# Fused attention and feed-forward layer: fp32 transposes in tiles of 64 rows, small work dealt to other places of the step

## The reference, cut to what matters

```
xn  = layernorm(x)                                  # x: 32 batches, 256 tokens, 128 channels, fp32
q, k, v = xn @ wq + bq, xn @ wk + bk, xn @ wv + bv  # 16 heads of 8 columns
att = softmax(q k^T / sqrt(8)) v                    # per head, 256 x 256 scores
prev = xn shifted by one token
r   = sigmoid((prev + mu_r (xn - prev)) @ W_r.T)
kk  = square(relu((prev + mu_k (xn - prev)) @ W_k.T))
y   = x + (att @ wo.T + bo) + r * (kk @ W_v.T)
```

## Time and profile before

| what | us |
|---|---|
| median of 3 runs (479.10 to 484.01) | 483.36 |
| the profiled execution | 477.82 |
| its span, first to last instruction | 476.0 |

### The profile page before, as it was taken

How to read it: one execution, slowest core, us unless ns; L and a number is a source line. 1 busy time by engine, 2 the same in 40 slices (tenths; PEclk the granted TensorE clock), 3 DMA queues, 4 the chain that set the end, 5 groups by cost and what they waited for, 6 DMA issues and landing times. The chain is left out here.

```text
span 476.0 us, 15644 instructions
## 1 busy us (share of the span) xinstructions
PE 444.1 (93%) x5238; PEld 272.0 (57%) x5238; DVE 402.4 (85%) x823; ACT 393.3 (83%) x866; POOL 367.9 (77%) x675
## 2 busy tenths in 40 slices
PE   5698999999999999999999999999999999999994
PEld 4244656565656656565666566566655565666541
DVE  7488898888989998899999888899998889988920
ACT  2047988989888898989888889898898898988883
POOL 6577888888878898788888888788897888876321
PEclk8579999999999999999999999999999999999998
DMA  4444355454344544453455454344554443445100
GB/s 142 134 125 125 104 147 157 127 147 141 111 122 145 156 141 138 121 145 113 127 154 149 139 148 124 102 142 135 156 154 124 149 127 111 129 135 147 47 15 22
DMA packets 85836, 60.42 MB, mean 127 GB/s; under 512 B 6192, under 2 KB 73392, under 8 KB 85808
## 3 DMA queue, kind: packets, MB, share of 16 engines
q1 hardware_dynamic: 85808, 60.06, 44.1%
HBM read 29.89 MB, written 29.36 MB: 124 GB/s over the span
## 5 line engine op out<-in xcount | busy, mean ns | idle before, releaser
L524 DVE TENSOR_REDUCE neg_max<-bank_max 128x2 f32<-128x512 f32 x512 | 328.2, 684 | 44.6 <-PE bank_max L645 40.1
L425 ACT ACTIVATE probs<-bank_exp 128x512 f32<-128x512 f32 x512 | 278.7, 600 | 25.4 <-PE bank_exp L635 24.1
L635 PE MATMUL bank_exp<-ops 51*128 51x256 bf16 x1024 | 156.9, 272 | 4.1 <-issue 3.0
L645 PE MATMUL bank_max<-ops 48*128 48x256 bf16 x1024 | 159.2, 276 | 0.0
L584 PE MATMUL bank_val<-probs,val 128*25 128x256 f32 x2048 | 138.1, 383 | 1.2 <-ACT probs L425 1.2
L635 PEld LDWEIGHTS bank_exp<-ops 51*128 51x128 bf16 x1024 | 75.0, 94 | 77.0 <-issue 65.2
L584 PEld LDWEIGHTS bank_val<-probs,val 128*25 128x25 f32 x2048 | 55.8, 103 | 41.6 <-issue 20.2
L645 PEld LDWEIGHTS bank_max<-ops 48*128 48x128 bf16 x1024 | 76.4, 95 | 5.2
L335 POOL TENSOR_SCALAR xn<-x_in,moments,rstd 128x128 f32<-128x128 f32 x62 | 49.4, 804 | 0.0
L374 POOL TENSOR_TENSOR mixed_x<-mixed_x,xn_t 128x512 f32<-128x512 f32 x32 | 40.7, 1272 | 2.5
L386 POOL TENSOR_TENSOR y<-projected,rest 128x256 f32<-128x256 f32 x32 | 23.4, 732 | 21.7 <-ACT projected L458 21.7
(11 more groups left out here) (67 smaller groups left out, 635.1 us busy)
## 6 DMA issues: line engine op xcount, KB each, us to landing
ops<-spill SPq DMA_DIRECT2D x128, 192.0 KB, 3.4
spill<-qk_h SPq DMA_DIRECT2D x64, 192.0 KB, 3.3
spill<-qk_m SPq DMA_DIRECT2D x64, 128.0 KB, 2.0
x_in<-x SPq DMA_DIRECT2D x32, 128.0 KB, 2.2
spill<-qk_l SPq DMA_DIRECT2D x32, 128.0 KB, 1.8
y_out<-y SPq DMA_DIRECT2D x32, 128.0 KB, 1.9
ops<-shift SPq DMA_DIRECT2D x128, 6.0 KB
w<-weights SPq DMA_DIRECT2D x1, 448.0 KB, 3.2
```

The source lines that it names most:

```text
L425: nc.scalar.activation(probs[g % 2][:, u % G, :, :], bank_exp[u % 2][:, :, :], ACT.Exp, scale=SCALE).then_inc(exp_done[u], 1)
L524: nc.vector.tensor_reduce(out=neg_max[hf][:, :, r, pr], in_=bank_max[MAX_BANK[v]][:, :, :], axis=AX_X, op=ALU.max, negate=True).then_inc(m ...
L635: exp_mm = nc.tensor.matmul(bank_exp[r][:, i, :], ops[p][rows, hf, 1, pr, i * P:(i + 1) * P], ops[p][rows, hf, 0, pr, :], start=True, stop ...
L645: max_mm = nc.tensor.matmul(bank_max[MAX_BANK[v]][:, i, :], of[rows, max_hf, 0, max_pr, i * P:(i + 1) * P], of[rows, max_hf, 1, max_pr, :] ...
```

## The change

All fp32 transposes (of `mixed`, `xn`, `att`) become two of 64 rows each: the upper 64 rows of the source go to `misc` bank 0, the lower to bank 1. Heads are ordered anew in `att` and in the weights to fit. The pieces move: the feed-forward product goes from u=7 to u=3, value and hidden product from u=11 to u=7, transposes of `xn` and `att` from u=7 to u=11, and the output projection in u=11 works on the batch before (t-2 instead of t-1). `transpose_shift` goes behind `mix_values` in u=1. On ACT the copies `val` and `act_r` go to u=7, and `xn_t`, `att_t` and `projected` to u=11, in that order. On DVE `ffn` goes to u=7 and the statistics to u=9. On POOL `rest` goes ahead of `qk_m`, `act_sq` goes behind `mixed_x` and is now for batch t+1, and `y` is for batch t-2. SP issues y out for batch t-2; its other transfers keep their order. The program has one step more at its end. In the diff, `near` and `far` are the two banks of `misc` by parity.

```
-        misc = [psum(f"misc{i}", [P, 2 * S]) for i in range(2)]
+        misc = psum("misc", [P, 2, 2 * S])
...
                     if u == 3 and live(0):
+
                         act.wait_ge(gate_psum, n(0))
+                        after(act, tokens_psum[0], n(-1))
+                        after(act, tokens_psum[1], n(-1))
                         after(act, ffn_done, n(-1))
...
+                    if u == 11 and (live(3) or live(-2)):
+
+                        after(act, xn_t_psum[0], n(3))
+                        after(act, xn_t_psum[1], n(3))
+                        after(act, att_t_psum[0], n(-1))
+                        after(act, att_t_psum[1], n(-1))
+                        after(act, wo_psum, n(-2))
+                        after(act, y_done, n(-3))
...
                     if u == 5 and live(-1):
-                        dve.wait_ge(tokens_psum, n(-1))
-                        nc.vector.reciprocal(inv_den[:, :], by_head[:, :, E]).then_inc(inv_done, 1)
+                        dve.wait_ge(tokens_psum[0], n(-1))
+                        dve.wait_ge(tokens_psum[1], n(-1))
+                        after(dve, gate_done, n(0))
+                        nc.vector.reciprocal(inv_den[:, :, :], by_head[:, :, :, E]).then_inc(inv_done, 1)
...
                     if u == 3 and live(0):
-                        pe.wait_ge(shift_done[1], n(0))
+                        after(pe, qk_rest_done[0], n(2))
...
+                        pe.wait_ge(shift_done[1], n(0))
+                        pe.wait_ge(act_sq_done, n(0))
+                        after(pe, mixed_done, n(-1))
+                        for i in range(ST):
+                            last = nc.tensor.matmul(near[:, S + i * D:S + (i + 1) * D], act_sq[:, i * P:(i + 1) * P],
+                                                    w[:, W_VV, :], start=True, stop=True)
+                        last.then_inc(ffn_psum, 1)
...
-                                last = nc.tensor.transpose(far[:, k * P:(k + 1) * P],
-                                                           mixed[:, i, st * P:(st + 1) * P], ident[:, :])
-                        last.then_inc(tokens_psum, 1)
+                                for r in range(2):
+                                    rows = slice(RG * r, RG * (r + 1))
+                                    last = nc.tensor.transpose(misc[:, r, k * RG:(k + 1) * RG],
+                                                               mixed[rows, i, st * P:(st + 1) * P], ident[rows, rows])
+                                    if k == 2 * ST - 1:
+                                        last.then_inc(tokens_psum[r], 1)
...
-                    if u == 11 and live(1):
-                        pe.wait_ge(shift_done[0], n(1))
+                    if u == 7 and live(1):
+                        after(pe, gate_done, n(0))
+                        after(pe, att_done, n(-1))
...
                         for i in range(ST):
                             last = nc.tensor.matmul(far[:, i * D:(i + 1) * D],
                                                     xn_t[(c + 1) % TURN][:, 1 + i * P:1 + (i + 1) * P], w[:, W_V, :],
...
+                    if u == 11 and (live(3) or live(-2)):
+                        after(pe, shift_done[0], n(1))
+                        after(pe, val_done, n(1))
+                        after(pe, act_r_done, n(1))
+                        after(pe, att_done, n(-1))
...
+                        if live(-2):
+                            pe.wait_ge(att_t_done, n(-2))
+                            for i in range(ST):
+                                last = nc.tensor.matmul(near[:, S + i * D:S + (i + 1) * D], att_t[:, i * P:(i + 1) * P],
+                                                        w[:, W_O, :], start=True, stop=True)
+                            last.then_inc(wo_psum, 1)
+                        if live(3):
+                            for i in range(ST):
+                                for r in range(2):
+                                    rows = slice(RG * r, RG * (r + 1))
+                                    last = nc.tensor.transpose(misc[:, r, i * RG:(i + 1) * RG], xn[rows, i, :],
+                                                               ident[rows, rows])
```

More of the change, by code:

```diff
@@ L341, in step @@
                     after(pool, spill_done, moved(1, SPILLS))
[L342 to L350, removed]
                 if live(-1):
@@ L381, in step @@
                     nc.gpsimd.tensor_tensor(rstd[:, :], var_eps[:, :], minus_half[:, :], ALU.pow).then_inc(rstd_done, 1)
[L382 to L387, removed]
+                if live(-2):
+                    pool.wait_ge(wo_done, n(-2))
+                    pool.wait_ge(rest_done, n(-2))
+                    after(pool, out_done[p], paired(-4))
+                    nc.gpsimd.tensor_tensor(y[p][:, :], projected[:, :], rest[p][:, :], ALU.add).then_inc(y_done, 1)
                 if live(1):
@@ L676, in step @@
                     if u == 5 and live(0):
                         mix_values(0, n(0), n(-1), p)
-                    if u == 7 and live(0):
-                        pe.wait_ge(act_sq_done, n(0))
-                        pe.wait_ge(gate_done, n(0))
-                        for i in range(ST):
-                            last = nc.tensor.matmul(near[:, i * D:(i + 1) * D], act_sq[:, i * P:(i + 1) * P],
-                                                    w[:, W_VV, :], start=True, stop=True)
-                        last.then_inc(ffn_psum, 1)
@@ L716, in step @@
                                          start=True, stop=True).then_inc(hidden_psum, 1)
-                    if u == 11 and live(-1):
-                        pe.wait_ge(att_t_done, n(-1))
+                    if u == 9 and live(0):
+                        mix_values(1, n(0), n(-1), p)
+                    if u == 9 and live(1):
+                        pe.wait_ge(max_split[0], n(1))
                         after(pe, ffn_done, n(0))
-                        after(pe, xn_t_done, n(3))
-                        for i in range(ST):
-                            last = nc.tensor.matmul(near[:, i * D:(i + 1) * D], att_t[:, i * P:(i + 1) * P],
-                                                    w[:, W_O, :], start=True, stop=True)
-                        last.then_inc(wo_psum, 1)
+                        if not live(0):
+                            after(pe, qk_rest_done[1], n(2))
+                            pe.wait_ge(consts_made, 2)
+                        transpose_shift(0, near)
```

175 lines of the change are left out of this document (93 added, 82 removed).

## The result

The changed kernel takes 504.0 us (median of 4 runs, 501.46 to 505.33), the kernel before 481.6 us (4 runs beside it): a ratio of 1.0459, 95% interval 1.0378 to 1.0541. It is slower, by about 22 us. The profiled execution took 501.46 us with a span of 499.4.

The account below looks back on a forecast made before the run. PE was taken to set the pace, DVE and ACT having 1.3 and 1.4 us to spare. 3.70 + 3.67 + 1.63 + 3.69 + 1.61 = 14.30 us a step, for 13.63, gave 497.6 as profiled, 499 us as median, 492 to 507.

Parts of the forecast that it names:

- A to B: PE time from the step's first pair of units (A, u=0 and 1) to the second: 1.63 us, before 2.00.
- E to F: PE time from the step's fifth pair of units to the sixth: 1.63 us, unchanged.
- B to C: PE time from second to third pair, with gate, feed-forward and halves: 2.07 us, before 1.62; gate waits for second qk_rest.
- Half transposes: PE's 64-row transposes, two side by side in 0.055 us: 0.37 for four whole ones' worth, against 0.53.
- rival of halves one at a time: Halves don't run side by side, so both places cost 0.59 us for 0.37: 511 us in all; chance 12%.
- C to E: PE time from third to fifth pair: 3.67 us, before 3.17; the value product waits for DVE's att.
- rival of a half hidden wait: The att wait ahead of the value product is half hidden, C to E loses 0.25 us: 483 to 490 us; chance 14%.
- PE's own 12.93: Rival: PE alone sets the pace, a 12.93 us step, 458 to 463 us; 12% together with only the att wait standing.
- F to A: PE time from sixth pair to the next step's first: 5.30 us, before 5.21; 3.69 to H (eighth pair), then 1.61.
- The rest: POOL's list, spills and SP's queue: costs nothing while the step stays over 13.6 us; at 12.9, cover 0.6 thinner.
- minus 1 for late loads: Two long steps before held 1 to 2 us of late loads that the longer step may hide: minus 1 us.
- the part carried over from profile to median: The runs' median lies 5.5 us above the profiled execution; part of it carried over, from 497.6 to 499 us.

Follow-up runs that it names:

- e6: Kernel before with only the shift transposes moved behind the mixed values (mix_values) in u=1: 476.19 us, ratio 0.9919.
- e8: Changed kernel with the shift transposes ahead of the mixed values again in u=1: 506.91 us, ratio 1.0575 to the kernel before.
- e3: Changed kernel with DVE making the second qk_rest in u=0 instead of u=1: 499.71 us, ratio 1.0395 to the kernel before.
- e2: Changed kernel with whole 128-row fp32 transposes again, everything else in its new place: 509.34 us, ratio 1.0629 to the kernel before.
- e1: Changed kernel with DVE making att in u=4 instead of u=5: 490.59 us, ratio 1.0214 to the kernel before.
- e12: e7 with y one step later on POOL, behind qk_l, and y out behind the loads on SP: 472.30 us, ratio 0.9852 to the kernel before.
- e4: Changed kernel with ACT copying projected in u=13 instead of u=11: 497.75 us, ratio 1.038 to the kernel before.
- e5: Changed kernel with the edits of e1, e3 and e4 together: 488.25 us, ratio 1.0175 to the kernel before.
- e7: e5 with ACT's copy of att_t moved from u=11 to u=13 too: 487.16 us, ratio 1.0166 to the kernel before.
- e9: e5 with y out issued one step later on SP, behind the last spill: 479.55 us, ratio 1.001 to the kernel before.
- e11: e9 with ACT's copy of att_t moved from u=11 to u=13: 472.70 us, ratio 0.9891 to the kernel before.

## Why the prediction was right

The forecast was 499 us, 492 to 507; the median is 504.0. The mechanism is borne out place by place: PE waits for DVE's att ahead of the value product and for ACT in H, and the step is 14.34 for 14.30.

**A to B**, and **E to F**: 1.63 and 1.63, as computed. e6 shows the 0.37 of A to B by itself. The gate's wait for qk_rest, which takes part of it back, stood in the next stretch of the prediction; e8 measures it.

**B to C**: 2.07 predicted, 2.06 measured, of terms that were each a little off: the gate starts 2.31 after A (2.34 predicted), gate 0.54 (0.55), feed-forward and halves 0.84 (0.81). In e3 they are 0.91, by the copy of mixed; that the feed-forward product stands close behind this copy is not in the prediction, and mattered only once the gate's wait was gone.

**Half transposes**: predicted at 0.37 for four whole ones' worth, with the changes of mode on both sides, against 0.53. In the changed kernel they take 0.84 - 0.44 = 0.40, e2's whole ones 0.54: 0.10 for the change ahead of the first half (0.54 from feed-forward to halves, 0.44 in e2) and 0.30 from there to C. Weight loads of the changed kernel by line (busy us, mean ns of one), to be set beside the earlier trace rows:

```profile
L698 PEld LDWEIGHTS misc<-ident,mixed 64*128 64x128 f32 x256 | 10.4, 138 | 4.9 <-ACT mixed L438 1.2
```

A load of 64 rows lasts 138 ns, a whole one 141, and still eight halves take less than four whole ones: two row groups do work side by side. The rule of the Trainium skill that was weighed ("TensorE: Matmul & The Clock Gate", LDWEIGHTS) would have made the halves no cheaper than 0.58 (0.15 + 4 x 0.107), dearer than the whole ones; e2 against the changed kernel shows 0.14 the other way. Its half that says that fewer rows don't shorten a load holds in the 138 ns. The rival of halves one at a time is out.

The price came out right, but the argument against that rule was not sound, and here luck helped. The prediction took 50 ns for 104 columns from the 141 and the 91 ns of the earlier trace rows, and these two loads differ in type as well, fp32 and bf16. Loads of one type, from the kernel before:

```profile
L635 PEld LDWEIGHTS bank_exp<-ops 51*128 51x128 bf16 x1024 | 75.0, 94 | 77.0 <-issue 65.2 <-ACT probs L425 2.8
...
L584 PEld LDWEIGHTS bank_val<-probs,val 128*25 128x25 f32 x2048 | 55.8, 103 | 41.6 <-issue 20.2 <-ACT probs L425 1.4
```

In bf16, 24 columns last 91 ns and 128 last 94. In fp32, 25 last 103 ns and the 128 of a transpose 141. Neither gives 50 ns, and the records overlap, so their length is not the distance at which they can follow each other. Whole transposes follow each other every 0.11 us, which is what the rule says too; it is only the halves, two every 0.06 us or so, that it doesn't fit.

**C to E**: 3.67 predicted, 3.66 measured; the wait for att was read from the earlier trace rows to 0.01 us, and e1 shows that it alone makes the difference. The rival of a half hidden wait is out too: DVE's first reduce still waits for PE, 0.45 after C (294.63 against 294.18). PE's own 12.93 came about in no kernel: e12 still has 2.00 in B to C for 1.90 and 1.81 in H to A for 1.61, both by ACT, and its step is 13.28.

**F to A**: 5.30 predicted, 5.36 measured. But the parts are not as they were put: H starts at 3.49 after F, 0.20 sooner than the 3.69, and H to A is 1.87 for 1.61. ACT's copies start at 1.93 after F, 0.10 later than the 1.83 predicted, and the wait for the second exponential falls inside the pair, between its two units (302.96 and 303.45), where the prediction had its first unit wait for all. e4 shows that the copies are the cause: with one of three gone, H comes 0.27 sooner.

**The rest**: "nothing, while the step stays over 13.6" held. In the changed kernel no wait for a load shows in the step. e4, e5, e7, e9 and e11 show the other half of that sentence: as soon as the step shrinks, or projected comes later, the loads of ops are late, by way of y on POOL and y out on SP. It was put as cover that would be 0.6 thinner; it cost e5 some 9 us (488.25 against e9's 479.55), all by which e5 was slower than the kernel before.

**The sum**: 28 x 0.67 = 18.8 was predicted, 28 x 0.71 = 19.9 came, and 404.92 - 383.95 = 21.0 in all. Missing from the prediction is the turn of the loop: it was in the trace of before, at 0.15 on PE's path, and the gate's new wait for DVE let it through at 0.72, 2.9 us more in five turns. The tail grew by 3.0 (49.7 for 46.67), 2 were predicted; the head shrank by 0.6. Together 23.4, which is the difference of the spans. The minus 1 for late loads was sound: two of the 28 steps of before ran 0.6 and 0.8 over 13.63 in G to H, and no step of the changed kernel is long there. The forecast of 497.6 for an execution like the profiled one met 501.46; the 3.9 between them are the turns, the 0.04 a step (1.1) and the tail (1.0), less some that the head and the first steps took off. The rest of the miss, 499 against 504.0, is in the part carried over from profile to median: 1.4 were put, 2.5 came.

## What to carry to other kernels

On an engine that sets the pace, a saved instruction is worth what the next wait leaves of it: here the halves themselves were a gain (e2), and two waits for engines with 1.3 us to spare made the step 5% longer. So when work is dealt anew, list for each piece the last thing that it waits for, at its new place, and move what produces it in the same edit; e1, e3, e4 and att_t in e11 are such moves, and with y out off the loads' path (e9) the change is a gain of 1.1 to 1.5% (e11, e12). When a step then gets shorter, look at once at the DMA queue: a store that waits at its head holds up every load behind it.

## What was not expected of the hardware

A turn of the hardware loop costs DVE some 0.4 us of "issue" in which it does nothing, and ACT starts its first copy 0.22 later there. It reaches PE in full only where PE waits for DVE just there: 0.15 before, 0.72 after, 0.21 to 0.28 in e3. The eight weight loads of the halves overlap, those of the two row groups and those of the pairs behind them. PE's loads in time in the changed kernel:

```profile
293.88 0.33 PEld L698 LDWEIGHTS misc<-ident,mixed 64*128 64x128 f32 x8
```

Eight loads of 138 ns would be 1.10 us one behind another, and all are done in 0.33.
